# Moving the transfers of the first heads, one behind each gather, in a fused attention and mixture kernel

## Chip, cores and metric

One Trainium2 chip, one of its cores. The metric is the time of one execution in device microseconds (us); the time of the kernel before is the median of three runs. The engines are PE (TensorE), DVE (VectorE), ACT (ScalarE), POOL (GpSimd) and SP (SyncE, which here only issues transfers); PEld is PE's weight load.

## What is computed

`x` is 4 x 1024 x 1024 in fp32. First a cross attention: `x`, layer-normalised along its rows and cut into 32 heads of 128 rows, gives the queries, and each head's 128 rows of `ctx` are keys and values. Then `x1 = x + gamma * attended` goes, layer-normalised, through a soft mixture of 8 low-rank experts. Cut to what matters:

```python
def _L0_xattn_ref(q, k, v, gamma):          # 8 heads in each of 4 batches: 32 of 128 rows
    qk = jnp.einsum('bhdq,bhdl->bhql', qh, kh) * scale
    sm = jax.nn.softmax(qk, axis=-1)
    ret = jnp.einsum('bhql,bhdl->bhdq', sm, vh)
    return gamma * ret.reshape(B, Dv, Lq)
...
x = x + _L0_xattn_ref(_layernorm(x, axis=-1), ctx_2048, ctx_2048, L0_xattn_gamma)
x = x + _L0_ffn_ref(_layernorm(x, axis=-1), L0_ffn_U, L0_ffn_V, L0_ffn_W1, L0_ffn_b1, L0_ffn_W2, L0_ffn_b2)
```

## The kernel before

Two stages follow each other: `attention` (up to about 775 us) and `mixture` (the rest). The change is in `attention` alone.

**Steps and heads.** A head is worked off in a slot of 8 steps (j = 0 to 7), one for each block of 128 queries. In a step PE makes 6 score matmuls (three products of high and low parts, two halves each) into one of two PSUM buffers `scores`, DVE takes the negated row maximum (`maxima`), ACT makes the exponentials `probs` with their sums (`exps`), and DVE turns `probs` into `pb` (`blocks`). A `scores` buffer is free for PE again when its exponentials are done: the matmuls of step s wait for `exps` of step s-2. In between, PE multiplies the values with the turned probabilities of earlier steps (`attended_products`, 12 steps behind), and ACT takes the result of each half head out of PSUM into `att_out` (`take_attended`, in steps j = 1 and j = 5, two heads behind). A half head is four steps.

**Gathers.** Every half head, SP issues 8 transfers of 256 KB from `pb` to `pt` (`gather`), which puts the turned probabilities where PE needs them. ACT rounds `pt` to `pt_hi` (`high_probs`, 9 steps behind), POOL subtracts to `pt_lo` (`low_probs`, 10 steps behind).

**SP's queue.** SP issues in the order in which `slot` of `sync` is written, and each issue waits in place for its semaphore. Besides the gathers these are `send_gain` (2 KB) and `store_attended` (256 KB from `att_out` to DRAM). Before `take_attended` overwrites a half of `att_out`, ACT waits until that half's previous store has landed: `act.wait_ge(s_att[half], h * 16)`. All transfers of SP and ACT share the core's 16 DMA engines.

**The own steps.** The mixture's first group of 4 tiles is prepared while attention still runs. `over_heads` makes heads 4 to 27 a hardware loop of 4 iterations (tile t) with 6 slots each (r = 0 to 5); below, "slot r3" is the fourth head of an iteration, and h9 is head 9 (its r is (h - 4) mod 6, so h9 is an r5). In them SP loads a half of `x` (`x_half`), the attended half (`own`) and its gains (`gain_row`), 256 KB each; DVE scales (`scale_own`), POOL adds (`add_residual`), DVE takes statistics (`own_statistics`, `own_variance`), POOL makes the factor (`own_factor`), ACT normalises in two parts (`normalise_own`) and SP stores `own` to `x1` and `own_in_order` to DRAM, 512 KB each. In the last head, `load_first` brings back what was stored in order. Behind the last gather SP issues the remaining stores of attended halves among the loads of the first weights (`w_raw`, L309 and L313); ACT takes head 31's half 0 there, then rounds the first weights (L1029), DVE subtracts (L1178), and the mixture's matmuls begin.

## Time and profile before

| | us |
|---|---|
| median of 3 runs (lowest to highest) | 1519.21 (1518.27 to 1520.94) |
| the profiled execution's own time | 1515.66 |
| its span, first to last instruction | 1513.9 |
| PE busy | 1476.6 (98%) |
| DVE busy, ACT busy, POOL busy | 1078.9, 822.8, 753.7 |

The profiled execution gives the rows below. Its page divides the span into 40 slices: DVE is at 9 tenths or more of each slice up to slice 20, where attention ends, and falls to 2 to 7 tenths in the mixture; the 16 DMA engines are busy 8 to 9 tenths of each slice of attention. The granted clock of PE is 1.00 throughout. A row of the timeline gives start and duration in us, engine, source line and operation, output and input; "SPq" is an issue from SP's queue, x8 that eight were merged, and what stands in square brackets is how long the engine had been idle and what released it.

### The profile page before, as it was taken

How to read it: one execution, taken by the hardware profiler on the slowest of the kernel's cores; microseconds unless marked ns; L12 is line 12 of the kernel's file. 1: busy time of each engine (PE TensorE's matmuls, PEld its weight loads, DVE VectorE, ACT ScalarE, POOL GpSimd, SP SyncE). 2: the span in 40 equal slices, each digit the busy share in tenths (PEclk: the TensorE clock that was granted, in tenths of full speed). 3: DMA queues.
4: the chain of work that ended last, by engine and by line, in shares of the span. 5: the costliest groups of instructions: out<-in, count | busy, mean ns of one | idle time of the engine just before them, and what ended most of it. 6: DMA issues, size and time to landing. Idle time of an engine off the chain costs nothing.

```text
span 1513.9 us, 20359 instructions
## 1 busy us (share of the span) xinstructions
PE 1476.6 (98%) x6176; PEld 1140.2 (75%) x6176; DVE 1078.9 (71%) x1303; ACT 822.8 (54%) x1262; POOL 753.7 (50%) x471
## 2 busy tenths in 40 slices
PE   5999999999999999999989999999999999999999
PEld 3777777777777777777767877778787887878877
DVE  7999999999999999999758646354564525545212
ACT  5888889889889888898763122111221212112110
POOL 2888988988889889888745201102011020200200
PEclk9999999999999999999999999999999999999999
DMA  5889999999999999998895563635537364463304
GB/s 163 256 276 296 290 283 289 288 289 297 292 282 297 291 290 295 280 292 269 260 362 177 187 205 117 229 123 194 196 116 245 121 203 162 143 218 125 112 1 139
DMA packets 144248, 338.65 MB, mean 224 GB/s; under 512 B 29440, under 2 KB 48896, under 8 KB 144192
## 3 DMA queue, kind: packets, MB, share of 16 engines
q1 hardware_dynamic: 126624, 290.31, 61.4%
q10 hardware_dynamic: 17568, 47.72, 9.2%
q8 instruction: 20, 0.33, 0.1%
q14 instruction: 36, 0.29, 0.1%
HBM read 136.36 MB, written 52.69 MB: 125 GB/s over the span
## 4 chain that ended last, share of the span: by engine, by line
PE 70%; DVE 11%; SPq 6%; issue 5%; DMA 4%; ACT 3%; ACTq 1%; POOL 0%; DVEq 0%; POOLq 0%
PE scores L1098 21%; PE scores L559 14%; PE attended L588 9%; PE attended L1147 9%; PE spare L1129 5%; PE scores L1129 5%; PE attended L591 4%; SPq L223 4%; DVE pb L633 3%; DVE neg_max L624 3%; DMA attended_rows<-att_out 2%; DMA pt<-pb 1%; PE scores L1113 1%; PE scores L1116 1%; ACT probs L435 1%
## 5 line engine op out<-in xcount | busy, mean ns | idle before, releaser
L345 POOL TENSOR_TENSOR pt_lo<-pt,pt_hi 128x512 fp32r<-128x512 f32 x254 | 478.8, 1897 | 98.4 <-ACT pt_hi L414 96.7
L435 ACT ACTIVATE probs<-scores,neg_max 128x1024 f32<-128x1024 f32 x256 | 285.4, 1115 | 87.5 <-DVE neg_max L624 82.0
L633 DVE STREAM_TRANSPOSE pb<-probs 128x1024 f32<-128x1024 f32 x256 | 315.8, 1234 | 11.4 <-DMA pt<-pb 5.8
L624 DVE TENSOR_REDUCE neg_max<-scores 128x1 f32<-128x1024 f32 x256 | 309.7, 1210 | 19.7 <-PE scores L559 18.8
L559 PE MATMUL scores<-k_hi,q_hi 128*128 128x512 f32 x512 | 210.9, 493 | 26.5 <-ACT probs L435 16.9
L414 ACT ACTIVATE pt_hi<-pt 128x512 fp32r<-128x512 f32 (+1 forms) x256 | 214.3, 837 | 7.0 <-DMA pt<-pb 7.0
L1044 ACT ACTIVATE hidden<-scores,b_col 128x512 f32<-128x512 f32 x64 | 44.1, 689 | 316.3 <-PE scores L1098 316.3
L993 POOL TENSOR_TENSOR rstd<-var_eps,minus_half 128x1 f32<-128x1 f32 x28 | 15.2, 550 | 397.8 <-DVE var_eps L1210 397.8
L1098 PE MATMUL scores<-nt_hi,w_hi 128*128 128x512 f32 x512 | 200.2, 391 | 1.3 <-DVE w_lo L1178 1.3
L1098 PE MATMUL scores<-nt_lo,w_hi 128*128 128x512 f32 x512 | 199.7, 390 | 0.0
L1098 PE MATMUL scores<-nt_hi,w_lo 128*128 128x512 f32 x512 | 199.4, 389 | 0.0
L1230 DVE TENSOR_TENSOR ht_lo<-hidden,ht_hi 128x512 fp32r<-128x512 f32 x64 | 48.8, 762 | 197.7 <-ACT ht_hi L1047 197.6
L559 PEld LDWEIGHTS scores<-k_hi,q_hi 128*128 128x128 f32 x512 | 92.8, 189 | 109.6 <-issue 61.0
L559 PE MATMUL scores<-k_lo,q_hi 128*128 128x512 f32 x512 | 159.6, 393 | 0.0
L559 PE MATMUL scores<-k_hi,q_lo 128*128 128x512 f32 x512 | 159.3, 392 | 0.0
L588 PE MATMUL attended<-pt_hi,v_hi 128*128 128x512 f32 x384 | 151.7, 395 | 1.5 <-POOL pt_lo L345 1.5
L588 PE MATMUL attended<-pt_lo,v_hi 128*128 128x512 f32 x384 | 150.6, 392 | 0.0
L588 PE MATMUL attended<-pt_hi,v_lo 128*128 128x512 f32 x384 | 150.0, 391 | 0.0
L591 PE MATMUL attended<-pt,v_nat 128*128 128x512 f32 x256 | 130.5, 591 | 0.0
L1002 POOL TENSOR_TENSOR nt_lo<-first_n,nt_hi 128x1024 fp32r<-128x1024 f32 x28 | 68.9, 2473 | 121.8 <-ACT nt_hi L1059 121.8
L1274 DVE TENSOR_TENSOR result<-attended,result 128x512 f32<-128x512 f32 x64 | 43.7, 683 | 106.2 <-DMA result<-x 64.2
L1098 PEld LDWEIGHTS scores<-nt_hi,w_hi 128*128 128x128 f32 x512 | 96.1, 188 | 28.2 <-issue 1.7
(103 smaller groups left out, 2599.1 us busy)
## 6 DMA issues: line engine op xcount, KB each, us to landing
pt<-pb SPq DMA_DIRECT2D x512, 256.0 KB, 5.2
attended_rows<-att_out SPq DMA_DIRECT2D x64, 256.0 KB, 5.4
result<-x SPq DMA_DIRECT2D x64, 256.0 KB, 4.3
out<-result SPq DMA_DIRECT2D x64, 256.0 KB, 3.0
k_raw<-in_ctx ACTq DMA_DIRECT2D x30, 512.0 KB, 5.3
x_raw<-in_x ACTq DMA_DIRECT2D x30, 512.0 KB, 6.4
first_n<-attended_rows SPq DMA_DIRECT2D x28, 512.0 KB, 4.0
gain_wide<-gains SPq DMA_DIRECT2D x28, 512.0 KB, 5.7
```

Source lines behind the costliest of these rows:

```text
L345: nc.gpsimd.tensor_tensor(pt_lo[2 * parity + half][:, :, keys, :], pt[2 * parity + half][:, :, keys, :], as_f32(hi[half][q][:]), ALU.subtr ...
L414: nc.scalar.activation(hi[half][q][:], pt[2 * parity + half][:, :, slice(*QUARTER_KEYS[q]), :], ACT.Copy).then_inc(s_pthi, 1)
L435: nc.scalar.activation(probs[j % 2][:], scores[j % 2][:], ACT.Exp, bias=neg_max[:, j:j + 1], accum_out=row_sum[b][:, j:j + 1]).then_inc(s_ ...
L559: last = mm(scores[j % 2][:, c * BANK:(c + 1) * BANK], q[b][:, queries], k[b][:, c * BANK:(c + 1) * BANK], start=(i == 0), stop=(i == 2))
L588: ins = mm(attended[half][:], v[b][:, key, :], moved, start=(q == 0 and i == 0), stop=(key == SPLIT - 1 and i == 2))
L591: ins = mm(attended[half][:], v_nat[b][:, q, :], pt[at][:, :, SPLIT + q, :], start=False, stop=False)
L624: nc.vector.tensor_reduce(neg_max[:, j:j + 1], scores[j % 2][:], AX_X, ALU.max, negate=True).then_inc(s_max, 1)
L633: nc.vector.transpose(pb[half][:, :, j % HALF, :], probs[j % 2][:]).then_inc(s_blocks, 1)
L1002: nc.gpsimd.tensor_tensor(tokens_of(nt_lo, k), gathered(k), as_f32(tokens_of(nt_hi, k)), ALU.subtract).then_inc(s_nlo, 1)
L1098: ins = mm(work[e % 2], w[:, k, cols[e]], n, start=(k == 0 and i == 0), stop=(k == KB - 1 and i == 2))
L1129: ins = mm(value_ps[r], w[:, d, r * P:(r + 1) * P], n, start=(d == 0 and i == 0), stop=(d == KB - 1 and i == 2))
L1147: ins = mm(y_ps[c], w[:, r, k * P:(k + 1) * P], u[:, r, c * BANK:(c + 1) * BANK], start=(r == 0 and i == 0), stop=(r == RB - 1 and i == 2))
```

## The change

The own steps' transfers and operations are placed anew in the six slots, and the two stores of attended halves are moved.

- SP, own loads: before, `load_own` issued `x_half`, `own` and `gain_row` together, behind the gain of half 0 in slots r0 and r2. Now each goes by itself directly behind a gather (`own` of half 0 and `x_half` of half 1 behind the gather of the previous head's half 1; the other four loads behind that of half 0), spread over r0 to r3.
- SP, own stores: `x1` is stored in r5 behind the first gather (before: at the end of r4), `in_order` still in r5, now ahead of the gain.
- SP, attended halves: half 0, taken in j = 1, is stored behind the next gather; half 1, taken in j = 5, likewise, in the same slot. Before, each waited one gather longer. In the last slot, the store of head 29's half 1 now stands ahead of `load_first` and of the last gather, and that of head 28's has gone to slot 30.
- DVE: `scale_own` moves from r1 and r3 to r2 and r4 (j = 4). `own_statistics` moves from j = 4 and j = 7 of r4 to j = 4 of r3 and j = 0 of r5; `own_variance` from j = 0 to j = 1 of r5.
- POOL: `add_residual` in j = 6 instead of 5, `own_factor` in j = 2 instead of 1.
- ACT: `normalise_own` in j = 4 and 5 of r5 instead of 3 and 5.

```diff
--- before.py
+++ after.py
@@ -233,16 +233,21 @@
             sp.wait_ge(s_att_out, h * 2 + b + 1)
             sp.dma_start(att[rows_of(h), b * BANK:(b + 1) * BANK], att_out[b][:]).then_inc(s_att[b], 16)
 
-        def load_own(t, b):
+        def own_residual(t, b):
 
             if b == 0:
                 sp.wait_ge(s_own_free, t * 32 + 16)
             else:
                 sp.wait_ge(s_added, t * 2 + 1)
             sp.dma_start(x_half[:], x[rows_of(t), b * BANK:(b + 1) * BANK]).then_inc(s_res_in, 16)
+
+        def own_attended(t, b):
             sp.wait_ge(s_att[b], t * 16 + 16)
             sp.dma_start(own[:, b * BANK:(b + 1) * BANK], att[rows_of(t), b * BANK:(b + 1) * BANK]
                          ).then_inc(s_own_in, 16)
+
+        def own_gains(t, b):
+
             sp.wait_ge(s_gain_out[b], 16 * FIRST)
             sp.dma_start(gain_row[:], scratch[bass.ds(t * 2 + b, 1), :].rearrange("a n -> (a n)")
                          .partition_broadcast(P)).then_inc(s_gain_in, 16)
@@ -263,31 +268,38 @@
                 sp.dma_start(first_n[k][:], in_order[bass.ts(k, P), :]).then_inc(s_f_in[k], 16)
 
         def slot(h, n, parity, first, last, own_step=None):
+
+            t, r = own_step or (None, None)
             known = isinstance(h, int)
             if not first:
                 gather(h - 1, n - JB, 1, 1 - parity)
-            if not (known and h < 3):
-                store_attended(h - 3, 1)
+            if r == 1:
+                own_attended(t, 0)
+            if r == 3:
+                own_residual(t, 1)
+            if r == 5:
+                store_own(t)
             if last:
                 load_first(n, (0, 1))
+
+            if not (known and h < 2):
+                store_attended(h - 2, 0)
             if not first:
                 send_gain(h - 1, 1)
-            if last:
-                store_attended(h - 2, 0)
             gather(h, n, 0, parity)
-            if not (known and h < 2 or last):
-                store_attended(h - 2, 0)
+            if r == 0:
+                own_residual(t, 0)
+            if r in (1, 3):
+                own_gains(t, r // 2)
+            if r == 2:
+                own_attended(t, 1)
+            if not (known and h < 2):
+                store_attended(h - 2, 1)
+            if r == 5:
+                store_own_in_order(t)
             send_gain(h, 0)
             if last:
                 load_first(n, (2, 3))
-            if own_step is not None:
-                t, r = own_step
-                if r in (0, 2):
-                    load_own(t, r // 2)
-                if r == 4:
-                    store_own(t)
-                if r == 5:
-                    store_own_in_order(t)
 
         load_x(0)
         load_k(0)
@@ -303,7 +315,6 @@
         h, n = over_heads(sp, slot)
         gather(h - 1, n - JB, 1, 1)
         send_gain(h - 1, 1)
-        store_attended(h - 3, 1)
         sp.wait_ge(s_gather[0], heads * GATHERS)
         for tile, dram in shared["w1_low_loads"]:
             sp.dma_start(tile, dram).then_inc(shared["s_w1_low"], 16)
@@ -368,9 +379,9 @@
                     scale_of_queries(h + 1, 1 - parity)
                 if j == 7 and not last:
                     low_values(h, parity)
-                if j == 5 and r in (2, 4):
+                if j == 6 and r in (2, 4):
                     add_residual(t, r // 2 - 1)
-                if j == 1 and r == 5:
+                if j == 2 and r == 5:
                     own_factor(t)
 
         nc.gpsimd.memset(minus_half[:], -0.5).then_inc(s_const, 1)
@@ -493,8 +504,8 @@
                 if j == 1 and not first:
                     act.wait_ge(s_vlo, h)
                     load_v(h)
-                if j in (3, 5) and own_step is not None and own_step[1] == 5:
-                    normalise_own(own_step[0], j // 2 - 1)
+                if j in (4, 5) and own_step is not None and own_step[1] == 5:
+                    normalise_own(own_step[0], j - 4)
                 if j == 6:
                     high_values(h, n, parity)
                 if j == 4 and more:
@@ -689,7 +700,7 @@
         def slot(h, n, parity, first, last, own_step=None):
             t, r = own_step or (None, None)
             for j in range(JB):
-                if j == 0 and r == 5:
+                if j == 1 and r == 5:
                     dve.wait_ge(s_own_stat, t * 2 + 2)
                 maxima(n + j, j)
                 if j == 3 and not last:
@@ -698,11 +709,11 @@
                     blocks(n - 1, JB - 1, h - 1)
                 elif j > 0:
                     blocks(n + j - 1, j - 1, h)
-                if j == 4 and r in (1, 3):
-                    scale_own(t, r // 2)
-                if (j, r) in ((4, 4), (7, 4)):
-                    own_statistics(t, j // 7)
-                if j == 0 and r == 5:
+                if j == 4 and r in (2, 4):
+                    scale_own(t, r // 2 - 1)
+                if (j, r) in ((4, 3), (0, 5)):
+                    own_statistics(t, r // 2 - 1)
+                if j == 1 and r == 5:
                     own_variance(t)
                 if j == 2 and not first:
                     inverse_sums(h - 1, 1, 1 - parity)
```

**SP, slot r2**, from the gather of half 0 on (`pt<-pb` is the gather; L234 the store of an attended half; L229 a gain). Rows that are only ISA or REGISTER_ALU are waits and address arithmetic. Before the first, in the changed kernel the second:

```order
L223 DMA pt_81<-pb_71 64x1x1024 x8
L234 ISA
L234 DMA attended_rows<-att_out_123 128x512
L228 ISA
L229 ISA
L229 DMA gains<-gain_139 128x4
L241 REGISTER_ALU
L242 ISA
L242 DMA x_half<-in_x 128x512
L244 DMA own<-attended_rows 128x512
L247 ISA
L247 DMA gain_row<-gains 128x512
```

```order
L223 DMA pt_81<-pb_71 64x1x1024 x8
L246 ISA
L246 DMA own<-attended_rows 128x512
L234 ISA
L234 DMA attended_rows<-att_out_124 128x512
L228 ISA
L229 ISA
L229 DMA gains<-gain_139 128x4
L219 REGISTER_ALU
L223 DMA pt_83<-pb_72 64x1x1024 x8
```

The three loads stood together behind the gain; now one load stands between the gather and the store, and the next gather follows the gain.

**ACT, slot r5**, from the end of step j = 3 to step j = 5. `probs` are the exponentials (`exps`), `q` and `q_hi` the next head's queries, `own_in_order` is `normalise_own`:

```order
L476 REGISTER_ALU
L477 ACTIVATE own_in_order<-own,own_shift,own_rstd 128x4x128
L432 REGISTER_ALU
L435 ACTIVATE probs_120,row_sum_136<-scores,neg_max 128x1024
L414 ACTIVATE pt_hi_3_76<-pt_81 128x1024
L501 REGISTER_ALU
L421 ISA
L421 DMA k_raw<-in_ctx 128x1024
L443 ACTIVATE q_99<-x_raw,q_shift_111,q_scale_107 128x1024
L450 ACTIVATE q_hi_89<-q_99 128x1024
L432 REGISTER_ALU
L435 ACTIVATE probs_121,row_sum_136<-scores,neg_max 128x1024
```

```order
L446 ACTIVATE probs_120,row_sum_136<-scores,neg_max 128x1024
L425 ACTIVATE pt_hi_3_76<-pt_81 128x1024
L487 REGISTER_ALU
L488 ACTIVATE own_in_order<-own,own_shift,own_rstd 128x4x128
L512 REGISTER_ALU
L432 ISA
L432 DMA k_raw<-in_ctx 128x1024
L454 ACTIVATE q_99<-x_raw,q_shift_111,q_scale_107 128x1024
L461 ACTIVATE q_hi_89<-q_99 128x1024
L443 REGISTER_ALU
L446 ACTIVATE probs_121,row_sum_136<-scores,neg_max 128x1024
```

The first `normalise_own` stood ahead of the exponentials of j = 4; now it stands behind them and ahead of the queries, so that both stand in the two steps around the queries.

**DVE, end of slot r4 and start of slot r5.** `neg_max` is `maxima`, `pb` is `blocks`. Before, the rows begin with `blocks` of r4's step j = 6 and hold j = 7 and the start of r5; in the changed kernel they begin in r5's step j = 0:

```order
L633 STREAM_TRANSPOSE pb_72<-probs_120 128x32x32
L663 REGISTER_ALU
L664 BN_STATS own_stats<-own 128x6
L623 REGISTER_ALU
L624 TENSOR_REDUCE neg_max<-scores 128x1
L633 STREAM_TRANSPOSE pb_72<-probs_121 128x32x32
L668 BN_AGGR own_mean_var<-own_stats 128x2
L669 REGISTER_ALU
L670 TENSOR_SCALAR own_neg_mean<-own_mean_var 128x1
L671 TENSOR_SCALAR own_var_eps<-own_mean_var 128x1
L637 ISA
L638 BN_STATS stats_101<-x_raw 128x6
```

```order
L674 REGISTER_ALU
L675 BN_STATS own_stats<-own 128x6
L648 ISA
L649 BN_STATS stats_101<-x_raw 128x6
L634 REGISTER_ALU
L635 TENSOR_REDUCE neg_max<-scores 128x1
L643 REGISTER_ALU
L644 STREAM_TRANSPOSE pb_71<-probs_120 128x32x32
L679 BN_AGGR own_mean_var<-own_stats 128x2
L680 REGISTER_ALU
L681 TENSOR_SCALAR own_neg_mean<-own_mean_var 128x1
L682 TENSOR_SCALAR own_var_eps<-own_mean_var 128x1
```

The statistics of half 1 stood in r4's last step; now they stand in r5's first, and the variance has gone one step on.

## Rows read from the trace of the kernel before

**Rows 1.** The page: busy time and share of each engine.

```profile
PE 1476.6 (98%) x6176; PEld 1140.2 (75%) x6176; DVE 1078.9 (71%) x1303; ACT 822.8 (54%) x1262; POOL 753.7 (50%) x471
```

**Rows 2.** Windows from a head's first `scores<-k_lo,q_hi` to another's: length, PE busy, clock, DMA.

```profile
98.95:657.72 558.77, 552.31 (x2210) 1.00 0.93 290
98.95:121.64 22.69, 22.69 (x93) 1.00 0.92 277
167.97:192.02 24.05, 22.99 (x93) 1.00 0.96 297
214.72:239.63 24.91, 23.72 (x94) 1.00 0.93 292
379.09:493.02 113.93, 113.93 (x461) 1.00 0.93 291
632.81:657.72 24.91, 23.85 (x94) 1.00 0.95 290
```

**Rows 3.** Waits of ACT for a store: total us, times, longest.

```profile
ACT att_out L397 <- DMA attended_rows<-att_out: 9.4, 6, 4.2
```

**Rows 4.** Timeline of SP, head 7 (an r3): r2's three loads and what follows.

```profile
171.61 0.43 SPq L242 DMA_DIRECT2D x_half<-in_x  x1
...
172.72 0.33 SPq L247 DMA_DIRECT2D gain_row<-gains  x1
173.16 8.45 SPq L223 DMA_DIRECT2D pt<-pb  x8
181.81 0.57 SPq L234 DMA_DIRECT2D attended_rows<-att_out  x1
```

**Rows 5.** Timeline of ACT, head 7, step j = 5.

```profile
189.56 0.60 ACT L397 ACTIVATE att_out<-attended 128x512 f32<-128x512 f32 x1 [1.68 <-DMA attended_rows<-att_out]
```

**Rows 6.** Timeline of SP, head 18 (an r2) before its loads.

```profile
436.98 0.81 SPq L234 DMA_DIRECT2D attended_rows<-att_out  x1
438.05 0.84 SPq L229 DMA_DIRECT2D gains<-gain  x1
439.67 8.55 SPq L223 DMA_DIRECT2D pt<-pb  x8
```

**Rows 7.** Timeline of ACT, head 21 (an r5), from step j = 3 on.

```profile
507.50 1.32 ACT L477 ACTIVATE own_in_order<-own,own_shift,own_rstd 128x512 f32<-128x512 f32 x1
...
508.61 1.07 ACT L435 ACTIVATE probs<-scores,neg_max 128x1024 f32<-128x1024 f32 x1
...
512.86 1.09 ACT L435 ACTIVATE probs<-scores,neg_max 128x1024 f32<-128x1024 f32 x1
```

**Rows 8.** Timeline of PE, head 21, step j = 7.

```profile
514.09 0.73 PE L559 MATMUL scores<-k_hi,q_hi 128*128 128x512 f32 x2 [0.78 <-ACT probs L435]
```

**Rows 9.** Timeline of DVE, head 21: the row maximum of step j = 4.

```profile
506.64 1.22 DVE L624 TENSOR_REDUCE neg_max<-scores 128x1 f32<-128x1024 f32 x1
```

**Rows 10.** Timeline of DVE, end of head 20 and start of head 21.

```profile
494.85 0.65 DVE L664 BATCH_NORM_STATS2 own_stats<-own 128x6 f32<-128x512 f32 x1
...
497.92 0.17 DVE L668 BATCH_NORM_AGGREGATE own_mean_var<-own_stats 128x2 f32<-128x12 f32 x1
...
498.25 0.69 DVE L638 BATCH_NORM_STATS2 stats<-x_raw 128x6 f32<-128x512 f32 x1
```

**Rows 11.** Timeline of POOL, head 19 (an r3, with `scale_own`) and start of 20.

```profile
460.99 5.72 POOL L345 TENSOR_TENSOR pt_lo<-pt,pt_hi 128x1024 fp32r<-128x1024 f32 x2
...
469.65 1.62 POOL L345 TENSOR_TENSOR pt_lo<-pt,pt_hi 128x512 fp32r<-128x512 f32 x1 [0.96 <-ACT pt_hi L414]
...
473.70 2.40 POOL L345 TENSOR_TENSOR pt_lo<-pt,pt_hi 128x1024 fp32r<-128x1024 f32 x1 [0.64 <-ACT pt_hi L414]
```

**Rows 12.** Timeline of PE: the product that reads the last `pt_lo` above.

```profile
477.19 0.40 PE L588 MATMUL attended<-pt_lo,v_hi 128*128 128x512 f32 x1
```

**Rows 13.** Timeline of ACT behind the last head: `take_attended` of head 31's half 0.

```profile
772.91 0.60 ACT L397 ACTIVATE att_out<-attended 128x512 f32<-128x512 f32 x1 [1.90 <-DMA attended_rows<-att_out]
```

**Rows 14.** Timeline of PE: the mixture's first matmul.

```profile
776.10 0.47 PE L1098 MATMUL scores<-nt_hi,w_hi 128*128 128x512 f32 x1 [1.30 <-DVE w_lo L1178]
```

## Prediction

> **What bounds the kernel now.** Read first the page's busy shares: PE is busy for 98% of the span [rows 1], so the time is PE's work plus the places where PE stands, and DVE, ACT, POOL and SP matter only where they hold PE up. The change is in attention, so the next view is one of windows, each from a head's first `k_lo` score matmul to the next head's. A head in which nothing holds PE takes 22.69 us [rows 2], the floor. The 24 heads of the loop take 558.77 us [rows 2]; 24 times 22.69 is 544.56, so PE loses 14.2 us in the whole loop. That is all that can be won there.
>
> Where are they? The heads in slot r5 take 24.91 us in the first iteration and 24.91 in the last, of 4 that lie within 0.2 [rows 2]: 2.2 to 2.4 lost in each, 9.2 in all. The other five heads of the third iteration take 113.93 [rows 2], 0.48 over 5 x 22.69: a quiet iteration. Four of these are 1.9. What is left, 14.2 - 9.2 - 1.9 = 3.1, was lost in single places, head 7 above all with 24.05 [rows 2].
>
> Head 7 says why. SP issued r2's three loads from 171.61 to 173.05, and only then the gather, so that the store behind it was issued at 181.81 [rows 4]. ACT must wait with `take_attended` of step j = 5 until this store has landed: it stood 1.68 us and began at 189.56 [rows 5]. Exponentials are queued behind it on ACT, and PE's scores wait for those. ACT waited for such a store 6 times in all, 9.4 us [rows 3]; two of these lie behind the last head, the longest among them.
>
> **The change, part by part.**
>
> *Stores of attended halves.* The store of half 1 is issued behind a gather of the slot in which it was taken, half a head earlier, about 11 us (22.69 / 2). Head 7's wait of 1.68 us [rows 5], the largest in the loop, is covered six times. These waits go even if the loads make a gather late. What do they give back? Of the 3.1 us I take 2.6, since some of the single losses may have another cause, such as the loop's jump back, that stays. Bounds: 1.4 (24.05 - 22.69, head 7 alone [rows 2]) and 3.1.
>
> *Own loads, one by one.* A load by itself stands between a gather and the next. In head 18 SP finished the gain at 438.05 + 0.84 = 438.89 and began the gather at 439.67 [rows 6]: 0.78 us of waiting for `blocks`. One load takes 0.33 to 0.43 us to issue [rows 4], so it fits. I take 0 for it. Before, three did not fit, and the gather moved; that harm is already in the stores' sum.
>
> *Scaling.* `scale_own` goes from r1 and r3 to r2 and r4. The quiet iteration has it in r1 and r3, both within the 0.48 us of five heads [rows 2]. r2 and r4 have the same two steps of room, in which DVE waits for ACT's exponentials behind the queries. 0 net.
>
> *Statistics and variance.* One `own_statistics` goes to r3's j = 4, where there is that room: 0. The other costs DVE 0.65 us, in r4's last step before, in r5's first one now; the variance takes 498.25 - 497.92 = 0.33 in either step [rows 10]. So DVE enters r5 earlier and has lost it again after one step. It has one step less in which PE's two buffers can even it out: I take +0.1 per iteration, between 0 and 0.3.
>
> *Normalising.* This is the part that costs. In r5, ACT is the engine that PE waits for: 0.78 us in step j = 7, released by exponentials [rows 8]. ACT runs through from `normalise_own` at 507.50 to the exponentials of j = 4 at 508.61 and those of j = 5 at 512.86 [rows 7]. So the normalising takes 1.11 us start to start, and the path from exponentials to exponentials, with the queries in it, 4.25. The row maximum of j = 4 was done at 506.64 + 1.22 = 507.86 [rows 9]. Without the normalising in front, the exponentials of j = 4 could begin at about 507.9, so 0.7 earlier. But then 1.11 is added behind them: 507.9 + 4.25 + 1.11 = 513.26, against 512.86. The exponentials of j = 5, for which PE stands, are 0.4 us later, and so is all behind them on ACT. The move gives its time to exponentials that nobody waits for, and takes it from the ones for which PE waits. +0.4 per iteration; with DVE's 0.1 it is +0.5, and 4 x 0.5 = +2.0. Bounds: 0, if PE had room, against which [rows 8] speaks, and 1.11 per iteration (4.4), if the exponentials of j = 4 didn't move forward at all.
>
> *POOL.* In r2 and r4 `scale_own` and `add_residual` now fall into one head. Beside `scale_own`, two low parts take 5.72 us instead of 2 x 2.40 [rows 11], 0.92 more. `add_residual` at j = 6 falls into POOL's idle 0.96 us [rows 11]. PE reads the `pt_lo` that ended at 473.70 + 2.40 = 476.10 only at 477.19 [rows 11, 12], and POOL had been idle 0.64 before it: 1.7 us of cover. 0.
>
> The Trainium skill, "SBUF — State Buffer", section "SBUF: two separate sides", says that a DVE instruction with two inputs in SBUF and a GpSimd instruction exclude each other from a shared pair of ports, and that the loser blocks for the whole instruction. By that rule each of the two low parts could be held up fully, and the 0.92 would be about double; whether the cover then holds is rival D. The row decides for the sum.
>
> *Behind the loop.* The store of head 29 leaves the queue between the last gather and the weights, so the store of head 30's half 0 can be issued up to about 0.8 us earlier. ACT waits 1.90 us for its landing before it can round the first weights [rows 13], and PE 1.30 us for their low part [rows 14]. But the last gather is now behind that store, and later by about 0.4, and as many bytes are ahead of it all. I take -0.2, between -1.3 (PE's whole wait) and +0.5. In the mixture nothing changes.
>
> The sum: -2.6 + 2.0 - 0.2 = -0.8 us, made against the profiled execution (span 1513.9, its own time 1515.66). That execution was 3.55 us faster than the median of 1519.21, to which I add the difference: **1518.4 us**. A measurement of this kernel tells about 0.2%, 3.0 us, from no change: I forecast no change.
>
> **Rivals.**
>
> *A. The late stores cost more than the profile shows (faster).* r1 and r3 of all four iterations have head 7's order on SP, three loads ahead of a gather; eight places, of which the profile shows few as late. The unprofiled runs are 3.5 us longer, which may be late stores in other iterations. One like head 7's costs 24.05 - 22.69 = 1.36 us [rows 2]. It decides from four such on: -5.4 + 2.0 - 0.2 = -3.6, 1515.6; five are -5.0, 1514.2; all eight -9.1, 1510.1. Against it: the third iteration shows none that PE felt.
>
> *B. The normalising costs nothing.* If the `normalise_own` in j = 4 found idle time, the loop would keep -2.6 - 0.2: 1516.4, near the border of faster. Rows 7 speak against it: ACT runs through.
>
> *C. The gathers come late in r1, r3 and r5 (slower).* SP has 0.78 us between gain and gather [rows 6]; a load takes 0.33 to 0.43, but issues of the same size took up to 0.84 here [rows 6], and in r5 the 512 KB store of `own` comes in between. DVE may overwrite `pb` only when the gather has landed. It decides once load and gap exceed 0.78 us: each 0.4 us too much, which PE would not hide where DVE has no room, in 3 slots x 4 iterations is 4.8 us, on top of -0.8: +4.0, 1523.2. For it: DMA engines that are 93% busy [rows 2]. Against it: a head has two steps of room.
>
> *D. POOL comes late (slower).* Were POOL held up by `scale_own` twice as much as in [rows 11], 0.92 us more, and `add_residual` not in idle time but on top, with at most the 1.62 us of the longest low part of its size [rows 11], it would be 2.5 us later; less the cover of 1.7 that is 0.8 us of PE in each r2 and r4, 6.4, and the time 1524.8. It decides from 1.7 us on. The rule of the Trainium skill on the shared ports speaks for it, the row's 0.92 against it.
>
> **Chances.** Forecast, no change: 0.57; A 0.22; B 0.10, split evenly between same and faster; C 0.09; D 0.02. So faster 0.27, same 0.62, slower 0.11. The range leaves out about 1 in 10 on each side: down to 1514.5, about where A with five late stores would be, up to 1521.5, where normalising at its bound of 4.4 would be (-0.8 + 2.4 = 1520.8) with a part of C. The likeliest case alone is 1517 to 1520.
>
> **What the new profile would show.** Right: no wait of ACT for a store inside the loop; r1 to r4 at 22.7 to 22.9 us each also in the first iteration; r5 at about 25.4 instead of 25.0, with the idle time of PE in j = 7 at 1.2 instead of 0.8 and ACT without a gap from the exponentials of j = 4 to those of j = 6; SP's gathers in r0 and r2 behind `blocks` at once. Wrong: an r5 that is no longer, or a head of r1 to r4 above 23.2 with DVE waiting for a gather or PE for `pt_lo`. The prediction fails if the medians hold much more of late stores than the profiled run, or if the loads make gathers late.

## The result, and the profile after

The changed kernel takes 1523.96 us (median of 20 runs, 1521.56 to 1526.70), against 1518.63 for the kernel before in the same session: ratio 1.0032, 95% interval 1.0024 to 1.0040. It is slower, 5.3 us where I had forecast 0.8 less. The profiled executions have spans of 1520.3 and 1513.9 us. Each is one execution: that of the kernel before took 1515.66 us, about 3 less than its medians, so a difference of two profiles can miss that of the medians by as much.

The windows by head of the changed kernel are laid as in [rows 2]: all 24 heads of the loop, head 7 (an r3), head 10 (an r0), head 19 (an r3) and head 21 (an r5).

```profile
98.93:665.72 566.79, 554.55 (x2209) 411.21 (x2208) 542.67 (x605) 497.89 (x776) 495.24 (x305) 1.00 0.92 285
167.04:190.74 23.70, 23.41 (x94) 17.04 (x92) 23.27 (x27) 20.34 (x33) 20.78 (x13) 1.00 0.90 282
239.97:264.48 24.51, 22.98 (x94) 17.20 (x92) 21.22 (x25) 20.64 (x33) 20.06 (x13) 1.00 0.91 276
451.41:475.08 23.67, 23.38 (x94) 17.05 (x93) 22.91 (x27) 20.37 (x33) 20.74 (x13) 1.00 0.87 274
498.21:524.68 26.47, 24.08 (x94) 16.82 (x92) 24.52 (x30) 22.33 (x35) 21.08 (x15) 1.00 0.89 272
```

The loop grew from 558.77 [rows 2] to 566.79, 8.0 us. Outside it 1.6 us were gained: 1520.3 - 566.79 against 1513.9 - 558.77. The loop's 8.0 summed by slot over the four iterations: r0 +1.2, r1 -0.7, r2 -1.3, r3 +2.1, r4 +1.0, r5 +5.7. The clock is 1.00 throughout. Every r3 is now about 23.7, every r5 26.3 to 26.5, and r1 and r2 are at their floor.

The waits, in total us, times and longest, first of ACT and then of PE:

```profile
ACT att_out L408 <- DMA attended_rows<-att_out: 6.7, 2, 4.1
...
PE scores L570 <- ACT probs L446: 20.1, 24, 1.8
...
PE scores L570 <- DVE q_lo L686: 2.0, 8, 0.3
```

ACT's waits for a store went from 9.4 us in 6 [rows 3] to 6.7 in 2, both behind the loop: the four in the loop are gone. New is the last line: PE waits for DVE's `q_lo` 8 times. That is the low part of the next head's queries, computed in step j = 6 from `q` and `q_hi`. Eight is once behind each r2 and r4 of four iterations.

POOL, DVE, ACT and PE at the end of head 18 (an r2) and the start of head 19, from the changed kernel's timeline:

```profile
449.81 1.29 POOL L363 TENSOR_TENSOR own<-own,x_half 128x512 f32<-128x512 f32 x1
...
450.10 2.08 DVE L686 TENSOR_TENSOR q_lo<-q,q_hi 128x1024 fp32r<-128x1024 f32 x1
...
451.06 2.26 POOL L356 TENSOR_TENSOR pt_lo<-pt,pt_hi 128x512 fp32r<-128x512 f32 x1
...
452.10 1.21 DVE L635 TENSOR_REDUCE neg_max<-scores 128x1 f32<-128x1024 f32 x1
...
452.23 0.73 PE L570 MATMUL scores<-k_hi,q_lo 128*128 128x512 f32 x2 [0.21 <-DVE q_lo L686]
...
453.35 1.11 ACT L446 ACTIVATE probs<-scores,neg_max 128x1024 f32<-128x1024 f32 x1 [1.88 <-DVE neg_max L635]
...
454.60 0.30 PEld L570 LDWEIGHTS scores<-k_hi,q_hi 128*128 128x128 f32 x2 [0.91 <-ACT probs L446]
```

`add_residual` (L363) started at 449.81 and ended at 451.10. `q_lo` started 0.29 us after it and took 2.08, where the shortest of its 32 instances takes 1.19. Take 1.19 from its end at 452.18 and it is 450.99, within 0.11 of the add's end: it did nothing until the add was through, and then ran unhindered. What it waited for is the rest of the add, not all of it. Behind the add stands `pt_lo`, 2.26 us where 1.30 is usual; 1.30 before its end at 453.32 is 452.02, about the end of `q_lo`: it was held in its turn. So the two engines took turns by whole instructions. What follows from it: the row maximum is late, ACT's exponentials stand 1.88 us for it, and the weight load of PE's score matmuls behind them 0.91.

The kernel before had the same turn-taking, with the low part of j = 6 in the add's place. Its head 19 is the third line:

```profile
444.59 1.30 POOL L345 TENSOR_TENSOR pt_lo<-pt,pt_hi 128x512 fp32r<-128x512 f32 x1
...
445.27 1.70 DVE L675 TENSOR_TENSOR q_lo<-q,q_hi 128x1024 fp32r<-128x1024 f32 x1
...
447.35:470.16 22.81, 22.81 (x93) 17.19 (x92) 22.78 (x26) 20.40 (x32) 20.40 (x13) 1.00 0.97 318
```

`q_lo` took 1.70 to 1.72 in each r2 and 1.48 to 1.72 in each r4, and PE waited for none of them: DVE had room in these heads, as `scale_own` wasn't in them. In the loops of both kernels there are 39 places where POOL is in an instruction when `q_lo` begins, and in each `q_lo` ends 1.08 or 1.09 us behind the end of that instruction. So two things came together in the change: `q_lo` is held longer (1.97 to 2.15), and DVE's room for it is gone.

r5's later half, on ACT and PE, answers to [rows 7] and [rows 8]:

```profile
514.11 1.12 ACT L446 ACTIVATE probs<-scores,neg_max 128x1024 f32<-128x1024 f32 x1 [0.29 <-DVE neg_max L635]
...
516.16 1.31 ACT L488 ACTIVATE own_in_order<-own,own_shift,own_rstd 128x512 f32<-128x512 f32 x1
517.27 1.20 ACT L454 ACTIVATE q<-x_raw,q_shift,q_scale 128x1024 f32<-128x1024 f32 x1
...
519.47 1.10 ACT L446 ACTIVATE probs<-scores,neg_max 128x1024 f32<-128x1024 f32 x1
```

```profile
520.71 0.73 PE L570 MATMUL scores<-k_hi,q_hi 128*128 128x512 f32 x2 [1.37 <-ACT probs L446]
524.14 0.70 PE L570 MATMUL scores<-k_hi,q_hi 128*128 128x512 f32 x2 [0.42 <-ACT probs L446]
```

From exponentials to exponentials it is now 519.47 - 514.11 = 5.36 us, which is the 4.25 of before plus one normalising of 1.11. PE stands 1.37 us in j = 7, 0.78 before [rows 8].

### The profile page after: what moved, and what is told of

It is laid out like the page before. It is cut to its first block, busy times and chain, and to the rows that moved or that the text cites. A ratio compares the mean times of both kernels' runs of the same rounds, so it can differ in the third digit from the quotient of the medians.

```text
span 1520.3 us, 20355 instructions
## 1 busy us (share of the span) xinstructions
PE 1478.1 (97%) x6176; PEld 1140.1 (75%) x6176; DVE 1082.8 (71%) x1303; ACT 823.2 (54%) x1262; POOL 758.6 (50%) x471
## 4 chain that ended last, share of the span: by engine, by line
PE 64%; DVE 17%; issue 7%; SPq 4%; ACT 3%; DMA 2%; ACTq 1%; POOL 0%; DVEq 0%; POOLq 0%
PE scores L1109 21%; PE scores L570 11%; PE attended L1158 10%; DVE pb L644 7%; PE attended L599 7%; PE spare L1140 5%; PE scores L1140 5%; DVE neg_max L635 5%; PE attended L602 3%; SPq L223 3%; DMA pt<-pb 1%; PE scores L1124 1%; PE scores L1127 1%; ACT probs L446 1%; DVE own L670 1%
## 5 line engine op out<-in xcount | busy, mean ns | idle before, releaser
L356 POOL TENSOR_TENSOR pt_lo<-pt,pt_hi 128x512 fp32r<-128x512 f32 x254 | 484.3, 1919 | 99.3 <-ACT pt_hi L425 97.7
```

The source lines that it names most:

```text
L356: nc.gpsimd.tensor_tensor(pt_lo[2 * parity + half][:, :, keys, :], pt[2 * parity + half][:, :, keys, :], as_f32(hi[half][q][:]), ALU.subtr ...
```

## The experiments

Twelve kernels, in three groups of four (x1 to x4, x5 to x8, x9 to x12), each group on another chip and timed against the kernel before, whose medians there are 1518.32, 1519.01 and 1519.49 us. "Under" and "over" are differences to that median. The ratio in brackets, with its 95% interval, is not that of the two medians, and the two can differ by up to 1.7 us (x4: 1.5 us under, ratio 1.0001), so of two kernels a difference under about 2 us tells nothing by itself. Edits are against the changed kernel unless said otherwise; their line numbers are left out.

### 1 to 3: the residual add and the normalising, each put back, and both

**x1_add_j5**

```diff
-                if j == 6 and r in (2, 4):
+                if j == 5 and r in (2, 4):
                     add_residual(t, r // 2 - 1)
```

> The changed kernel, with add_residual back in step j = 5 of r2 and r4. Theory P (ports): at j = 6 the add on POOL pushes POOL's next low part onto DVE's q_lo, which took 2.08 us there instead of 1.19 to 1.72, and PE stands for q_lo and then for the row maxima behind it; moved back, q_lo takes 1.2 to 1.7 us in r2 and r4, the r3 heads come down from 23.67 to about 22.8 us and the r5 heads from 26.4 to about 25.5, so 5 to 7 us less than the changed kernel: about 1518. Rival S (scaling): what costs is that scale_own now stands in r2 and r4 at all, whatever POOL does: less than 1.5 us off, about 1523. Rival G (late gathers in r1, r3, r5): likewise unchanged, 1523 to 1524.

**x2_norm_j35**

```diff
-                if j in (4, 5) and own_step is not None and own_step[1] == 5:
-                    normalise_own(own_step[0], j - 4)
+                if j in (3, 5) and own_step is not None and own_step[1] == 5:
+                    normalise_own(own_step[0], j // 2 - 1)
```

> The changed kernel, with normalise_own back in steps j = 3 and 5 of r5. Theory N (the step of the prediction): the exponentials of j = 5 come 0.5 us earlier in each r5, 2.0 us over the loop: about 1522. Rival: ACT has room there, no difference, 1524. If the first iteration's long jump (r0 at 24.50 us in the changed kernel) hangs on where ACT's work ends, up to 1.7 us more come back, 1520.3.

**x3_both_back** has both edits.

> The changed kernel with both moved back: add_residual in j = 5, normalise_own in j = 3 and 5. Under P and N the gains add up to 7 to 9 us: 1515 to 1517, which is 0.1 to 0.25% faster than the kernel before. Under S or G with N: about 1521 to 1522.

Measured: x1 1516.23 (ratio 0.9986, 0.9974 to 0.9997), x2 1521.28 (1.0026, 1.0015 to 1.0036), x3 1515.36 (0.9988, 0.9977 to 1.0000). Moving one POOL instruction of 1.3 us by one step takes the kernel from 5.3 us over to 2.1 under, 7.4 in all (7.0 by the ratios 1.0032 and 0.9986). Heads 19 and 21 of x1:

```profile
447.23:470.28 23.05, 23.05 (x93) 17.12 (x92) 22.22 (x27) 20.55 (x33) 20.08 (x13) 1.00 0.94 299
493.06:518.80 25.74, 23.77 (x94) 16.90 (x92) 23.76 (x30) 22.31 (x35) 20.34 (x15) 1.00 0.91 281
```

Its `q_lo` in r2 and r4 takes 1.36 to 1.43: it meets the low part of j = 6, as in the kernel before, but later in it. Of x2 and x3, r5 alone:

```profile
495.59:521.67 26.08, 24.11 (x93) 16.81 (x92) 24.53 (x30) 22.21 (x35) 21.12 (x15) 1.00 0.85 266
```

```profile
492.56:517.91 25.35, 23.74 (x93) 16.90 (x92) 23.78 (x30) 22.21 (x35) 20.37 (x15) 1.00 0.88 273
```

The normalising's move costs 26.47 - 26.08 = 0.39 us an iteration with the add in j = 6, and 25.74 - 25.35 = 0.39 with it in j = 5. I had worked out 0.4. In the medians, 4 x 0.39 = 1.6 us stands beside 2.4 (x2) and 0.9 (x3 against x1). The add is the large one.

### 4 and 8: the order on SP

**x4_stores_only** is the kernel before with nothing but the new way of the attended halves' stores: loads in threes behind the gain, and all own operations at their old places.

```diff
-            if not (known and h < 3):
-                store_attended(h - 3, 1)
...
+            if not (known and h < 2):
+                store_attended(h - 2, 0)
...
-            if last:
-                store_attended(h - 2, 0)
...
-            if not (known and h < 2 or last):
-                store_attended(h - 2, 0)
+            if not (known and h < 2):
+                store_attended(h - 2, 1)
...
-        store_attended(h - 3, 1)
```

> The kernel before, with nothing of the change but the stores of the attended halves (each behind the gather of its own half head, head 29's second one ahead of the last gather). The own loads stay together in r0 and r2. If the late stores are the whole of what single places lose (2.6 of 3.1 us) and the weights behind the loop come 1 us earlier: 3 to 4 us faster than before, about 1515. Rival: the later second gather behind a store takes it back, 0 to 1 us, 1518. ACT should not wait for a store inside the loop.

Measured: 1516.80 (1.0001, 0.9990 to 1.0012), 1.5 under, no change that can be told. Expected were 3 to 4 under. No wait of ACT for a store is left in the loop, and still head 7 takes 23.79 us. In it DVE waits twice for a gather, and PE stands twice for exponentials behind the second:

```profile
174.01 1.25 DVE L630 STREAM_TRANSPOSE pb<-probs 128x1024 f32<-128x1024 f32 x1 [0.41 <-DMA pt<-pb]
186.99 1.25 DVE L630 STREAM_TRANSPOSE pb<-probs 128x1024 f32<-128x1024 f32 x1 [0.78 <-DMA pt<-pb]
...
187.51 0.73 PE L556 MATMUL scores<-k_hi,q_hi 128*128 128x512 f32 x2 [0.25 <-ACT probs L432]
190.82 0.70 PE L556 MATMUL scores<-k_hi,q_hi 128*128 128x512 f32 x2 [0.30 <-ACT probs L432]
```

A late gather can thus cost PE with no store concerned. That the three loads make it late isn't shown. DVE waited for gathers 13 times here, 8.7 us in all, but x1, whose loads stand apart, has 12.8 us in 16. Nor does such a wait always cost: in x3, DVE stood longer in the same head, and the head took 22.96 us:

```profile
185.59 1.25 DVE L644 STREAM_TRANSPOSE pb<-probs 128x1024 f32<-128x1024 f32 x1 [1.51 <-DMA pt<-pb]
```

There the head holds a statistic of 0.65 us where x4 has `scale_own` with 2.12, so DVE had more room; that this is the reason is argued and not tested.

**x8_loads_together** is x3_both_back with the six loads in threes, behind the stores of r1 and r3:

```diff
-            if r == 1:
-                own_attended(t, 0)
-            if r == 3:
-                own_residual(t, 1)
...
-            if r == 0:
-                own_residual(t, 0)
-            if r in (1, 3):
-                own_gains(t, r // 2)
-            if r == 2:
-                own_attended(t, 1)
...
+            if r in (1, 3):
+                own_residual(t, r // 2)
+                own_attended(t, r // 2)
+                own_gains(t, r // 2)
```

> x3_both_back with the own loads together again, three behind the gain of half 0, in r1 and r3 (the latest place in time for scale_own), the stores of attended halves as changed. Theory G (three loads together make a gather about 0.9 us late, and that holds DVE or ACT even where no store is waited for): 2 to 4 us slower than x3_both_back, 1517.5 to 1519.5. Rival, the prediction's reading (only the store behind the gather mattered): as x3_both_back, 1515.4.

Measured: 1516.95 (0.9992, 0.9981 to 1.0003), 2.1 under, where x3 is 3.0 under. The loop is 560.48 us against 558.58. Expected were 2 to 4 us more than x3 if the grouped loads do harm and none if they don't; the medians' difference of 0.9 us is less than these intervals can tell, so this stays open.

### 5 to 7: lock, lateness, or the step

**x5_before_add_j6** is the kernel before (and its SP order) with one edit: `add_residual` in j = 6. `scale_own` stays in r1 and r3.

```diff
-                if j == 5 and r in (2, 4):
+                if j == 6 and r in (2, 4):
                     add_residual(t, r // 2 - 1)
```

> The kernel before, with nothing changed but add_residual in j = 6 instead of 5 (here r2 and r4 hold no scale_own). Theory P (the add on POOL and q_lo on DVE exclude each other): q_lo in r2 and r4 rises from 1.2 to 1.7 us towards 2.1 here too; without scale_own DVE has some room in these heads, so 0.3 to 0.8 us in each, 2.5 to 6 us in all: 1521 to 1524. Rival: only scale_own and add_residual in one head do harm, then no difference, 1518.5.

Measured: 1519.55 (1.0006, 0.9995 to 1.0018), no change that can be told. r5 stays at 24.87 to 25.02. In its head 18 POOL and DVE meet the other way round, and in head 19 a second pair meets:

```profile
447.02 1.71 DVE L675 TENSOR_TENSOR q_lo<-q,q_hi 128x1024 fp32r<-128x1024 f32 x1
447.60 2.28 POOL L352 TENSOR_TENSOR own<-own,x_half 128x512 f32<-128x512 f32 x1
...
463.88 2.77 DVE L659 TENSOR_TENSOR own<-own,gain_row 128x512 f32<-128x512 f32 x1
```

In head 18 `q_lo` is first, and it is the add that waits, 2.28 us instead of 1.29; nobody reads its result soon, and head 19's first step stays at 2.93 us. So the add in j = 6 doesn't by itself delay `q_lo`. In the changed kernel `scale_own` stands in the same head, DVE comes to `q_lo` later, when the add has begun, and the order comes out the other way. The add isn't free here either. In the r3 heads `scale_own` takes 2.51 to 2.78, where it took 2.24 to 2.32 before, and each of them is 0.5 to 1.0 us longer: head 19 takes 23.8 instead of 22.8 us. That is the whole of the 3.2 us by which the loop grew, to 561.97 in this profile; the medians show 0.5. Whether the add sets that second delay up wasn't tried apart.

**x6_memset**: in the changed kernel the residual add is cut to one column, and two memsets stand in its place, which read nothing from SBUF. The residual is missing from the result.

```diff
-            nc.gpsimd.tensor_tensor(half, half, x_half[:], ALU.add).then_inc(s_added, 1)
+            one = slice(b * BANK, b * BANK + 1)
+            nc.gpsimd.tensor_tensor(own[:, one], own[:, one], x_half[:, 0:1], ALU.add)
+            nc.gpsimd.memset(x_half[:, 1:BANK], 0.0)
+            nc.gpsimd.memset(own[:, b * BANK + 1:(b + 1) * BANK], 0.5).then_inc(s_added, 1)
```

> The changed kernel, whose add_residual in j = 6 is taken out but for one column: two memsets of 511 columns stand in its place on POOL, about as long (1.0 to 1.2 us together), so the residual is not added and the first group's rows are others. Theory P-lock (two inputs in SBUF on DVE against a POOL instruction that reads SBUF): q_lo starts in the memsets and isn't held by them, 1.2 to 1.5 us instead of 2.1; about as good as add_residual in j = 5, 1516 to 1518. Rival P-queue (POOL's next low part comes late and falls on q_lo, whatever stands before it): q_lo stays at about 2 us and the time at 1523 to 1524.

Measured: 1514.42 (0.9966, 0.9954 to 0.9979), 4.6 under, and below the 1516 to 1518 that I expected. POOL is still busy with them while `q_lo` runs; the last two lines are heads 19 and 21:

```profile
445.37 0.20 POOL L364 TENSOR_TENSOR own<-own,x_half 128x1 f32<-128x1 f32 x1
445.50 0.53 POOL L365 MEMSET x_half<- 128x511 f32 x1
...
445.67 1.18 DVE L689 TENSOR_TENSOR q_lo<-q,q_hi 128x1024 fp32r<-128x1024 f32 x1
445.96 0.53 POOL L366 MEMSET own<- 128x511 f32 x1
...
446.95:469.75 22.80, 22.80 (x93) 17.15 (x92) 21.90 (x26) 20.40 (x33) 19.90 (x13) 1.00 0.89 297
492.52:518.07 25.55, 23.57 (x94) 16.89 (x93) 23.57 (x29) 22.32 (x35) 20.20 (x15) 1.00 0.88 279
```

Same place in POOL's queue, same start beside it, and `q_lo` takes its 1.18. Both memsets run beside it at their own 0.53. So it isn't that POOL has work in j = 6, but that this work reads SBUF while a DVE instruction with two inputs there wants to start. From the first start to the last end the three take 1.12 us, the add 1.29, so POOL's queue is hardly shorter for it. DVE's turning of `probs`, which has one input, takes 1.22 to 1.26 us in all 256 instances of x4, whatever POOL does.

**x7_add_j7** keeps the add whole and moves it past `q_lo`, with the normalising in j = 3 and 5:

```diff
-                if j == 6 and r in (2, 4):
+                if j == 7 and r in (2, 4):
                     add_residual(t, r // 2 - 1)
-                if j in (4, 5) and own_step is not None and own_step[1] == 5:
-                    normalise_own(own_step[0], j - 4)
+                if j in (3, 5) and own_step is not None and own_step[1] == 5:
+                    normalise_own(own_step[0], j // 2 - 1)
```

> normalise_own in j = 3 and 5 as before, and add_residual in j = 7 of r2 and r4, behind the low part and ahead of v_lo, all else as changed. P-lock: q_lo, at the start of POOL's idle time in j = 6, takes 1.2 to 1.5 us; the add then falls on row maxima and transposes, which have one input, and holds up nothing on DVE: as x3_both_back or up to 1.5 us better, 1514 to 1515.5. Rival: v_lo and the next low parts come 1.3 us later than PE's cover of 1.1 us, PE stands for pt_lo in r3 and r5, 1517 to 1520.

Measured: 1515.10 (0.9968, 0.9955 to 0.9980), 3.9 under; x2, which differs from it in the add's step alone, was 3.0 over on its chip. Head 19 and head 21:

```profile
446.43:469.21 22.78, 22.78 (x93) 17.18 (x92) 22.40 (x26) 20.45 (x33) 21.04 (x14) 1.00 0.95 298
491.99:517.13 25.14, 23.58 (x93) 16.90 (x92) 23.50 (x29) 22.34 (x35) 21.41 (x16) 1.00 0.92 294
```

Its `q_lo` takes 1.18 to 1.19 in r2 and r4. Set beside it, the head behind grows by what `q_lo` grows: r3 by 23.67 - 22.78 = 0.89 in the changed kernel with `q_lo` 2.08 - 1.18 = 0.90, by 23.05 - 22.78 = 0.27 in x1 with 1.43 - 1.18 = 0.25; r5 by 26.08 - 25.14 = 0.94 from x7 to x2, both with normalising in 3 and 5. DVE has no room left there: it sets the pace of these steps.

### 9 to 12: what is left in r5, and a better order

**x9_stat_back** is x3_both_back with the second statistic and the variance at their old places; the first statistic stays in r3.

```diff
-                if j == 1 and r == 5:
+                if j == 0 and r == 5:
                     dve.wait_ge(s_own_stat, t * 2 + 2)
...
-                if (j, r) in ((4, 3), (0, 5)):
-                    own_statistics(t, r // 2 - 1)
-                if j == 1 and r == 5:
+                if (j, r) in ((4, 3), (7, 4)):
+                    own_statistics(t, r - 3)
+                if j == 0 and r == 5:
                     own_variance(t)
```

> The change with both edits undone that the runs so far tell of (the residual add in the half head j=5, the normalising in j=3 and j=5), and now with the statistic of the own rows' second group back in r4's last half head and the variance back in r5's first. What is left of the change is the way of the stores, the gathers and the scaling. Theory that the place of statistic and variance costs about 0.3 us in each iteration: r5 of the undisturbed iteration goes from 25.35 (x3_both_back) to about 25.05, the median from 1515.4 to about 1514.2. Rival, that what r5 has over before is the scaling's new place: r5 stays at 25.3 to 25.4 and the median within 0.5 us of x3_both_back's distance to the kernel before (about 3 us less).

Measured: 1517.18 (0.9978, 0.9965 to 0.9991), 2.3 under. Head 21:

```profile
495.41:520.99 25.58, 24.18 (x94) 16.81 (x93) 24.02 (x30) 22.30 (x35) 20.45 (x15) 1.00 0.84 274
```

The theory fell: r5 grew from 25.35 to 25.58 instead of shrinking, by 0.22 to 0.25 in three of the four iterations (the last one lost 0.5). The rival's figure of 25.3 to 25.4 fell too. By the profiles the new place of statistic and variance is the better one, by 0.23 an iteration; x10, with the same old places, has 0.20 to 0.26 over x3 in all four. The medians can't tell it: by them x9 is 0.7 us slower than x3, by the ratios 1.5 us faster.

**x10_mixed** is x9_stat_back with the add in j = 7 for r2 alone: `(j, r) in ((7, 2), (5, 4))`.

> Normalising in j=3 and j=5; the residual add in j=7 for r2 and in j=5 for r4; statistic and variance back at their old places. Theory of the lock: an add whose run doesn't meet VectorE's q_lo costs nothing there, so q_lo in r2 takes 1.2 and in r4 1.4; r3 is 22.8 to 23.0 and r5 about 25.0; the median is that of x9_stat_back within 1 us, and about 4 to 5 us under the kernel before. Rival, that an add in j=7 pays at the start of the next head: r3 over 23.2 and the median over x9_stat_back's by more than 1 us.

Measured: 1515.92 (0.9980, 0.9965 to 0.9994), 3.6 under, where 4 to 5 were expected. `q_lo` takes 1.21 to 1.25 in r2 and 1.34 to 1.41 in r4; r3 is 22.78 to 22.81. Expected so; but r5, which has the statistic at its old place, is 25.4 to 25.6 and not 25.0.

**x11_norm_j36** is x7_add_j7 with the second normalising one step later.

```diff
-                if j in (3, 5) and own_step is not None and own_step[1] == 5:
-                    normalise_own(own_step[0], j // 2 - 1)
+                if j == 3 and own_step is not None and own_step[1] == 5:
+                    normalise_own(own_step[0], 0)
                 if j == 6:
                     high_values(h, n, parity)
+                if j == 6 and own_step is not None and own_step[1] == 5:
+                    normalise_own(own_step[0], 1)
```

> x7_add_j7 with the second normalising in j=6 and no longer in j=5, and the first in j=3. Theory that r5's excess over 22.69 is ScalarE's queue in j=4 to 7, which the normalising lengthens where ScalarE has no idle time behind it: r5 goes from 25.17 to about 24.6, and the median is about 2 us under that of x7_add_j7 (some 1513). Rival, that the projection of the own rows is then late and what is gained in r5 is lost behind it, at the start of r0: r0 of the later iterations longer by 0.5 or more and the median within 1 us of x7_add_j7's.

Measured: 1514.34 (0.9962, 0.9946 to 0.9979), 5.2 under, the fastest of the twelve. Head 21:

```profile
491.36:515.89 24.53, 23.33 (x93) 16.97 (x92) 22.87 (x29) 21.57 (x35) 21.92 (x16) 1.00 0.90 276
```

r5 lost 25.14 - 24.53 = 0.61, as expected. Its distance to before is 1.2 us more than x7's where 2.3 were gained in the loop's four r5, and the two intervals overlap. The rival's road isn't seen: the r0 of the three later iterations take 70.9 us together, 71.0 in x7. In the profiled run DVE waited 10.8 us in 13 waits for gathers, x7 4.7 in 10, and the two heads behind the loop took 23.5 each instead of 22.7. The second isn't the normalising's doing: x6, with both in j = 4 and 5, had 23.5 and 23.4 there. For the first, one profile doesn't tell.

**x12_mixed_norm** is x10_mixed with x11's normalising.

> x10_mixed with the normalising in j=3 and j=6. If both theories hold their gains add: r3 22.8 to 23.0, r5 24.4 to 24.6, the median 1512 to 1513.5, the best of all. Rival: what is gained in r5 goes into the start of r0, and the median is that of x10_mixed.

Measured: 1515.67 (0.9970, 0.9954 to 0.9986), 3.8 under: no more than x10_mixed or x7_add_j7. r5 was 24.6 to 24.9 in three iterations and 25.8 in the first. The gains didn't add up. The three later r0 take 70.0 us here and 69.3 in x10, too little for the rival to have taken them. In its profile 3.0 us more than in x10 lie outside the loop; why stays open.

## Why the prediction was wrong

**POOL, forecast 0: this step failed.** I wrote that `add_residual` "at j = 6 falls into POOL's idle 0.96 us", with 1.7 us of cover until PE reads `pt_lo`. The cover held: in the loop PE never stood for `pt_lo`. But I asked only what the add does to POOL's own queue, and not which DVE instruction it would then run beside. It ran beside `q_lo`, which took 1.97 to 2.15 us, against 1.18 unheld (x6, x7) and 1.48 to 1.72 before, when DVE had room for it. That is 0.9 us in each r3 and r5 of four iterations, 8 x 0.9 = 7.2 us; these eight heads are 7.0 us shorter in x6. In the medians, undoing the add's step gave 7.4 (x1) and 6.9 (x2 against x7), and x6 gave 9.9. By its `q_lo`, x1 should have given 5.6, so these figures agree to 2 or 3 us and no closer. The cost is about the whole miss of 5.3 + 0.8 = 6.1 us.

**Scaling, forecast "0 net": wrong with it.** I gave r2 and r4 the same room as r1 and r3. But in r2 and r4 `q_lo` already took 1.48 to 1.72, where it took 1.18 to 1.22 in r1 and r3, and they also hold the add. In x5, where `scale_own` isn't in these heads, the add in j = 6 makes no difference in r5. With `scale_own` DVE enters `q_lo` with no room, and every tenth of `q_lo` arrives at PE. The 0.25 of `q_lo` that x1 and x3 still have over 1.18 shows as 0.27 in their r3.

**Rival D.** It ended near the measured time (1524.8 against 1523.96), but by another road: it took POOL to be held up and PE to wait for `pt_lo`, 0.8 us in each r2 and r4. What was held up for PE's purposes was DVE. That its time came out is luck; I had given it 0.02. The rule that stands beside it did speak truly. The Trainium skill, "SBUF — State Buffer", section "SBUF: two separate sides", says that the loser blocks for the winner's whole instruction. This trace agrees in both directions: `q_lo` 0.9 behind the add, `pt_lo` 0.96 behind `q_lo` (2.26 against 1.30); and x6, whose memsets read nothing, shows no block. My "0.92 speaks against it" misread [rows 11], for I left out the row of DVE beside it:

```profile
462.11 2.31 DVE L659 TENSOR_TENSOR own<-own,gain_row 128x512 f32<-128x512 f32 x1
```

The first low part ended at 463.41, and `scale_own` at 464.42, 1.01 later; in all eight places of that kernel it is 0.97 to 1.02. So `scale_own` itself takes about 1.0 us, and the rest of its 2.31 is waiting for the first low part. The second low part took 3.36 instead of 2.40, which is `scale_own`'s 1.0 in full. The row bears the rule out, with one instruction held once, and neither of my readings of it.

**Late stores, -2.6: the sum about right, the cause not shown.** The waits went, as forecast. In x7, where `q_lo` isn't held in r2 and r4, r1, r2 and r3 together are 3.2 us shorter over four iterations than before. But x4 takes away the same waits, and there they are 0.5 us longer, with head 7 at 23.79. So the gain comes with the loads apart or the scaling moved, which I took at 0; x3 and x8, which differ in the loads alone, differ by 0.9 us in the medians and 1.9 in the loop of the profiles, and don't settle it. Rival A wanted 5.4 us or more from the stores' new way. x4, which is that alone, is 1.5 under by the medians and not under by the ratio: A isn't borne out. Why the profiled execution of the kernel before was 3.5 us faster than its median stays open.

**Gathers late (rival C):** not seen. In the changed kernel r1 and r2 stand at 22.69 to 22.73 in all four iterations, and DVE waited 8 times for a gather, 4.6 us, where before it was 15 times, 5.8 us. That count moves by itself: with the same transfers in the same order it is 12.8 us in x1, whose r1 and r2 are within 0.3 us of the floor. (The 0.84 us that I took from [rows 6] for an issue of a load's size is that of a gain; a store of that size took 0.81.)

**Normalising, +0.4:** right, 0.39 twice, and PE's idle time in j = 7 1.37 where I said 1.2.

**Statistics and variance, +0.1 between 0 and 0.3:** outside the bounds. By x9 the new place gives 0.23; r5 of x7 is nevertheless 0.09 over before (25.14 against 25.05), so by subtraction scaling in r4 costs r5 about 0.3, which no run tried by itself. Two of my terms were each off by 0.3 and cancelled. x3's further 0.2 is `q_lo` again.

**Behind the loop, -0.2:** -1.6 outside the loop in the profile, outside the bounds by 0.3. But what lies outside the loop takes 953.6 to 957.8 us in the twelve experiments, and 953.6 in the changed kernel. The distance from head 31's first score matmul to the mixture's first is 1.0 shorter (50.29 to 49.25), but runs from 48.0 to 51.1 over the twelve experiments, eleven of which issue the stores in the same order there. That term can't be told from noise.

**Not in the sum:** r0 lost 1.2 us more, nearly all of it in head 10 (below). And I held that this kernel shows a difference only from 3.0 us on; the interval of the result is 1.2 us to either side.

## What to carry to other kernels

When an instruction is moved on GpSimd, read which VectorE instructions stand beside its new place, not only whether GpSimd has room: if one has two inputs in SBUF, count the rest of the other's run, up to a whole instruction, as a wait for whichever begins second, and ask if that one is on the path. A step with room loses it when other work moves into the same stretch, so moves that are harmless one by one have to be priced together. Where an engine's queue bounds a stretch, extra work belongs behind the last instruction for which others wait in it (the normalising in j = 6), not into the step with the most idle time of its own.

## What the runs showed of the hardware

**Durations in a trace hold the wait for the other engine.** `q_lo`, always the same work, is listed with 1190/1470/2146 ns (shortest, median, longest). None of it appears as idle time. The comparison with an instruction's shortest instance is what shows it, if one instance ran free: of `scale_own` none did, and 2.10 us is its shortest for about 1.0 us of work.

**The jump back of the loop.** In head 10 (r0, 24.51 us) ACT stood 3.16 us and is said to have waited for a row maximum:

```profile
241.13 1.19 DVE L635 TENSOR_REDUCE neg_max<-scores 128x1 f32<-128x1024 f32 x1
...
241.62 1.05 ACT L425 ACTIVATE pt_hi<-pt 128x1024 fp32r<-128x1024 f32 x1
...
245.82 1.11 ACT L446 ACTIVATE probs<-scores,neg_max 128x1024 f32<-128x1024 f32 x1 [3.16 <-DVE neg_max L635]
```

That maximum was there at 242.32, and ACT was free at 242.67; nothing that the profile shows held it until 245.82. These are the exponentials of r0's step j = 0, ACT's first instruction behind its jump back. There is a pattern: behind the jump back (heads 10, 16 and 22) they begin 0.98 to 3.64 us after their row maximum, in all 42 places of the 14 kernels. In head 4, where the loop is entered, and in head 28 behind it, they begin 0.1 to 0.3 us after it. PE hides about the first 1.7 us: head 10 lost 0.53 us with 2.20 before the change and 1.82 with 3.50 after. In the 14 kernels these heads lost 0 to 2.0 us each. So the wait goes with the jump back, its size varies between runs of like kernels, and no run was made to tell its cause.
